# Attention statistics through a ring, and the scaling of probabilities one step later

## The reference

```
h = embed(x, position)
y = layernorm(h)
q, k, v = latent projections of y, with rope and rms norm      # 8 heads, 2 key/value heads, width 64
scores = einsum("bhqd,bhkd->bhqk", q, k) * 64 ** -0.5          # causal mask
attn_w = softmax(scores)
h = h + (einsum("bhqk,bhkd->bhqd", attn_w, v) + v_res) @ W_O
h = h + experts(layernorm(h))       # mean and variance of each token of h are needed here
```

## Time and profile before

| | |
|---|---|
| median of 3 runs | 2085.62 us (2084.45 to 2085.73) |
| the profiled execution | 2084.88 us |
| its span | 2083.0 us |
| TensorE busy | 1844.9 us (89%) |
| VectorE busy | 1828.0 us (88%) |
| ScalarE busy | 1454.8 us (70%) |
| GpSimd busy | 682.5 us (33%) |
| mean granted TensorE clock | 0.937 |
| `attend` in the trace | about 290 to 571 us |

### The profile page before, as it was taken

How to read it: one execution, slowest core, us unless ns; L and a number is a source line. 1 busy time by engine, 2 the same in 40 slices (tenths; PEclk the granted TensorE clock), 3 DMA queues, 4 the chain that set the end, 5 groups by cost and what they waited for, 6 DMA issues and landing times.

```text
span 2083.0 us, 29167 instructions
## 1 busy us (share of the span) xinstructions
PE 1844.9 (89%) x8486; PEld 1461.0 (70%) x8486; DVE 1828.0 (88%) x2358; ACT 1454.8 (70%) x2558; POOL 682.5 (33%) x439
## 2 busy tenths in 40 slices
PE   5455658878766999999999999999999999999998
PEld 3333335555554888888888888878888888888887
DVE  8435558888677999999999999979999999999997
ACT  2145546666522888888888888878888888888886
POOL 4250015445312233333333333323333333333330
PEclk9967769899955999999999999999999999999999
DMA  7410000000012333333333333323333333333331
GB/s 207 136 41 0 1 1 1 0 0 0 1 34 96 126 121 108 124 126 126 113 113 126 126 124 109 119 101 126 117 112 124 126 126 111 116 126 126 123 108 56
DMA packets 105256, 191.46 MB, mean 92 GB/s; under 512 B 13558, under 2 KB 86246, under 8 KB 88550
## 3 DMA queue, kind: packets, MB, share of 16 engines
q1 hardware_dynamic: 103166, 186.77, 26.1%
q0 software_dynamic: 2048, 4.20, 0.7%
HBM read 179.40 MB, written 11.53 MB: 92 GB/s over the span
## 4 chain that ended last, share of the span: by engine, by line
PE 67%; DVE 0%; issue 0%; ACT 0%; DVEq 0%; ACTq 0%
PE f_ps_h L1837 11%; PE f_ps_h L1838 11%; PE f_ps_h L1839 11%; PE f_ps_y L1848 11%; PE f_ps_y L1849 11%; PE f_ps_y L1850 11%; PE f_ps_y L1863 0%; DVE s_lo L1793 0%; DVE scaled L1787 0%; PE f_ps_h L1874 0%; ACT act_out L1748 0%; DVE h L1811 0%; ACT y_t L1772 0%; DVEq L1669 0%; PE f_ps_h L1819 0%
## 5 line engine op out<-in xcount | busy, mean ns | idle before, releaser
L1748 ACT ACTIVATE act_out<-f_ps_h,b_t 128x512 f32<-128x512 f32 x1024 | 649.6, 686 | 257.4 <-PE f_ps_h L1839 257.4
L1787 DVE TENSOR_TENSOR scaled<-act_out,c_row 128x1024 f32<-128x1024 f32 x512 | 753.0, 1471 | 42.7 <-ACT act_out L1748 42.2
L1793 DVE TENSOR_TENSOR s_lo<-scaled,s_hi 128x1024 fp32r<-128x1024 f32 x512 | 672.7, 1314 | 0.1
L1756 ACT ACTIVATE s_hi<-scaled 128x1024 fp32r<-128x1024 f32 x512 | 541.9, 1058 | 2.3 <-DVE scaled L1787 1.5
L1651 POOL CAST w_hi<-w_raw 128x512 fp32r<-128x512 f32 x128 | 200.7, 1568 | 909.8 <-PE f_ps_y L1850 898.0
L1837 PE MATMUL f_ps_h<-x_hi,w_hi 128*128 x1024 | 399.8, 390 | 2.2 <-DVE h L1811 1.5
L1848 PE MATMUL f_ps_y<-s_hi,w_hi 128*128 128x512 f32 x1024 | 398.7, 389 | 3.0 <-DVE s_lo L1793 3.0
L1838 PE MATMUL f_ps_h<-x_lo,w_hi 128*128 x1024 | 399.4, 390 | 0.0
L1839 PE MATMUL f_ps_h<-x_hi,w_lo 128*128 x1024 | 399.2, 390 | 0.0
L1850 PE MATMUL f_ps_y<-s_hi,w_lo 128*128 128x512 f32 x1024 | 398.4, 389 | 0.0
L1849 PE MATMUL f_ps_y<-s_lo,w_hi 128*128 128x512 f32 x1024 | 398.4, 389 | 0.0
(11 more groups left out here) (219 smaller groups left out, 1652.7 us busy)
## 6 DMA issues: line engine op xcount, KB each, us to landing
c_row<-comb_rows SPq DMA_DIRECT2D x128, 1024.0 KB, 4.8
w_raw<-in_w SPq DMA_DIRECT2D x256, 128.0 KB, 4.3
by_slot<-b_zeros SPq DMA_DIRECT2D x1, 3072.0 KB, 13.4
b_gauss_s<-by_slot SPq DMA_DIRECT2D x12, 256.0 KB, 5.3
mixed_rows<-b_mixed SPq DMA_DIRECT2D x12, 256.0 KB, 2.3
out<-h SPq DMA_DIRECT2D x8, 256.0 KB, 4.7
cent<-in_centers SPq DMA_DIRECT2D x1, 1536.0 KB, 7.1
neg_prec<-in_logvar SPq DMA_DIRECT2D x1, 1536.0 KB, 10.9
```

What stands on the lines that cost most here:

```text
L1748: last = act.activation(act_out[:, r % 2, c, :], ps_h[:, r % 2, c, :], ACT.Gelu, bias=b1_t[:, c, bass.ds(e, 1)])
L1756: act.activation(s_hi[:, r % RING], scaled[:, r % RING], ACT.Copy).then_inc(hi_ready, 1)
L1787: dve.tensor_tensor(scaled[:, r % RING], act_out[:, r % 2], c_row[:, k, g * GT:(g + 1) * GT].unsqueeze(1).broadcast_to([P, HC, GT]), ALU.m ...
L1793: dve.tensor_tensor(s_lo[:, r % RING], scaled[:, r % RING], s_hi[:, r % RING].bitcast(F32), ALU.subtract).then_inc(lo_ready, 1)
```

## The change

`statistics` keeps BN_STATS and BN_AGGR on VectorE, but BN_AGGR writes into one of four slots of a ring, `mv_ring`, and nothing waits behind it at once. ScalarE copies the whole ring (8 elements per partition) into `mv` every fourth step, at the head of steps 9, 13, ... 33, and once after the last step. BN_STATS waits also for the aggregate before, and the aggregate of slot 0 for the last copy of the ring. GpSimd's `norm_p` works in step u on unit u-3, no longer on u-2. TensorE's, ScalarE's and VectorE's other work is as it was.

```diff
-        mvt = sb("a_mvt", [P, 2])
+        mv_ring = sb("a_mv_ring", [P, 4, 2])
...
-        mv_step = sem("mv_step")
+        stats_ready = sem("stats_ready")
+        mv_ready = sem("mv_ready")
+        mv_copied = sem("mv_copied")
...
+            def copy_mv(u):
+                if in_range(u, UNITS):
+                    act.wait_ge(mv_ready, u + 4)
+                    act.activation(mv[:, bass.ds(u, 4), :], mv_ring[:], ACT.Copy).then_inc(mv_copied, 1)
+
             def step(u, r):
+                if r == 1:
+                    copy_mv(u - 9)
                 copy_p(u - 4, r, 0)
...
             all_steps(act, step)
+            copy_mv(UNITS - 4)
...
                 norm_qk(u + 2, (r + 2) % 4)
                 copy_v(u - 3, (r - 3) % 4)
-                norm_p(u - 2, (r - 2) % 4)
+                norm_p(u - 3, (r - 3) % 4)
...
-            def statistics(u):
+            def statistics(u, slot):
                 if in_range(u, UNITS):
-                    link = chained(dve, mv_step, u * 3)
                     hold(dve, y_added, u + 1)
-                    link(dve.bn_stats(stats[:], h[:, u, :]))
-                    link(dve.bn_aggr(mvt[:], stats[:]))
-                    link(dve.tensor_tensor(mv[:, u, :], mvt[:], mvt[:], ALU.max))
+                    if not isinstance(u, int) or u > 0:
+                        hold(dve, mv_ready, u)
+                    dve.bn_stats(stats[:], h[:, u, :]).then_inc(stats_ready, 1)
+                    if slot == 0:
+                        after(dve, mv_copied, u // 4)
+                    hold(dve, stats_ready, u + 1)
+                    dve.bn_aggr(mv_ring[:, slot, :], stats[:]).then_inc(mv_ready, 1)
```

More of the change, by code:

```diff
@@ L1275, in step @@
                 add_y(u - 5)
-                statistics(u - 5)
+                statistics(u - 5, (r - 5) % 4)
             all_steps(dve, step)
```

## The result

| | before | changed |
|---|---|---|
| median | 2085.68 us (2084.45 to 2085.87, 4 runs) | 2039.73 us (2036.94 to 2039.97, 4 runs) |
| ratio | | 0.9778, 95% interval 0.9763 to 0.9794 |
| span of the profiled execution | 2083.0 us | 2037.8 us |
| VectorE busy | 1828.0 us | 1773.0 us |
| TensorE busy | 1844.9 us | 1829.7 us |

The forecast was 2043.5 us, in a range from 2037 to 2058.

A forecast was written before the change was run, and what follows sets the result against it. VectorE leads in the attention stage, its copy to mv held by GpSimd's scaling. Pairs of 7.74 + 5.75 = 13.5 us instead of 16.65, with the edges, save 42.3 us: 2043.5 us, range 2037 to 2058.

The forecast's parts named there:

- The mechanism: VectorE's two-element copy to mv, up to 2968 ns, is held until GpSimd's norm_p ends; work behind it waits.
- The odd step: Attention step with twice the keys: 4.14+1.87+0.49+1.24 = 7.74 us from its score, set by TensorE.
- The even step: Attention step with half the keys: 5.75 us, set by GpSimd's scaling, which the next step's turn_p waits for.
- VectorE's own way: Even step, from copy_q through maximum, mask, add_y and BN_AGGR to the next copy_q: 5.4 us.
- The sum: Attention stage: 13 pairs at 13.5 us give −40.9; with step 31, startup and end, −42.3 us.
- The end of step 31: Last odd step: copy_o starts 6.2 us after its score instead of 8.3, −2.1 us.
- The startup: First steps of the stage: norm_p(1) now stands behind a norm_qk, +0.5 us at most.
- The end: After the last step, with ScalarE's eighth ring copy exposed, and the barrier: +0.2 us.
- GpSimd's move: Even step: norm_p on unit u-3 is late behind norm_qk's wait for turn_q; without this gate −5 us more.
- ScalarE's part: Eight ring copies, 0.2 us each taken (0 to 1.02); seven covered by odd-step idle, the eighth exposed.
- the rival's price: TensorE's clock drops to 1.2 GHz in every pair: about 1.7 us each, 23 in all, 2066 us; chance 0.07.
- The slower rival: VectorE's copies, maximum and mask held while norm_p runs: pair 18.6 against 16.65 us, +25 us, 2111 us; chance 0.03.

The follow-up runs named there:

- the reduce in its place: Kernel before the change, with VectorE's two-element TENSOR_TENSOR copy to mv replaced by a TENSOR_REDUCE over an axis of one; ratio to before 0.9788.
- the tensor_copy: Kernel before the change, with VectorE's two-element TENSOR_TENSOR copy to mv replaced by a tensor_copy; ratio to before 1.0004.
- the two-input kernel: Changed kernel plus a two-element TENSOR_TENSOR from SBUF on VectorE, behind the maximum of every step; ratio to the kernel before 0.9948.

## Why the prediction was right, point by point

**The mechanism** was right. The held copy was the loss; the reduce in its place shows it without the rest of the change, and the tensor_copy shows that the place is not the cause.

**The odd step** was forecast at 7.74 us, set by TensorE, and is 7.58. Every offset up to the start of `turn_p` is as worked out (4.14, 1.87, 0.49). The term that was mis-sized is the last: from `turn_p`'s start to the free TensorE I took 1.24 us, and it is 1.08 (409.61 to 410.69). I had added durations whose modelled ends overlap by more than I allowed; two starts, had I shown them, would have been safer.

**The even step** was forecast at 5.75 us with GpSimd's scaling late, and is 5.60 with just that wait (0.34 us before `turn_p`). `turn_p` follows the scaling by 0.06 us, where I had 0.1 to 0.2, and the score follows `turn_p` by 1.13 where I had 1.24. VectorE's own way, 5.4 us, is what the step takes when GpSimd's wait is gone: 5.40.

**The sum.** The pair is 13.14 and not 13.5 us, 4.7 us over 13 pairs. The end of step 31 came out as forecast: its `copy_o` starts at 501.03, 6.20 us after the score (6.2). The startup cost nothing where I had allowed 0.5: the first two pairs take 10.83 and 9.71 us, before 10.84 and 9.72. The end cost nothing either: from the last BN_AGGR to routing's first instruction, with ScalarE's last ring copy between, 0.74 us against 0.93. So the stage gave 47.6 us for 42.3 of the sum. Against it stand 2.6 us ahead of the stage, where the two kernels do not differ. The changed kernel's profile has a slow stretch of the clock in the embedding that the other has not. The same window in the kernel before, and in the changed one:

```profile
84.00:88.00 4.00, 4.00 (x39) 4.00 (x38) 2.09 (x4) 1.80 (x4) 0.00 (x0) 1.00 0.71 215
```

```profile
84.00:88.00 4.00, 4.00 (x23) 4.00 (x22) 1.38 (x2) 1.19 (x2) 0.00 (x0) 0.57 0.60 176
```

TensorE is busy for all of both, but gets through 23 matmuls in place of 39. At the last copy of this part (90.92 before, 93.27 now) 2.35 of the 2.61 us are there. Of these, 0.71 us stand already ahead of the slow stretch, at a copy behind a DMA (81.31 and 82.02), so the slow stretch is worth about 1.6. What set the drop off I did not try. One of the four runs, 2036.94 us, lies about as much below the others, which fits a drop that comes in some executions only; this was not shown. That the time came within 4 us of the forecast is in part luck: the stage gave 5 us more than its sum, and 2.6 us that have nothing to do with the change hid half of that. Without them the time would have been about 2037 us, the lower edge of the range.

**GpSimd's move** I called what is late next, and gave 5 us for it. Its price is 3.3 us of the stage, shown twice: by undoing it, and by taking away the wait ahead of it. Nor does ScalarE's part cost anything in the loop: of its eight ring copies only the last, behind the last step, waits for its aggregate.

**The rivals.** The clock did not drop: it is 1.00 from 320 to 495 us. I gave no row for the rival's price, 1.7 us a pair; the two-input kernel shows 0.7 to 1.1, and what a slow stretch would cost in the changed kernel was not measured. Every slow stretch of the loops came with a long idle of TensorE ahead of it (2.63 us in the two-input kernel, 1.6 to 2.1 us before), while the gaps of 0.2 to 0.4 us in the changed kernel set off none in 175 us. The Trainium skill ("TensorE: Matmul & The Clock Gate", A second HAM failure mode) speaks of frequent micro-idles that make the clock oscillate; that is not borne out here at this size of gap. But the long idle alone does not decide: two pairs of the two-input kernel have the same 2.63 us and no drop, and neither has the kernel before from 420 to 498 us, with idles of 1.64 to 2.12 us in each pair. What else it takes is open. In the kernel before the drops cost nothing that shows: neighbouring pairs alternate between 16.55 and 16.91 us, with and without them. Two windows of that kernel, the first with drops (columns as in the earlier trace rows):

```profile
347.00:420.00 73.00, 62.65 (x412) 42.86 (x413) 62.52 (x84) 47.28 (x165) 36.08 (x27) 0.88 0.00 1
420.00:498.00 78.00, 59.55 (x438) 40.82 (x435) 67.46 (x89) 50.56 (x169) 40.17 (x29) 1.00 0.00 0
```

The slower rival needed maximum, mask or copies to be held. None is; what would be held is shown by the added instruction, and with it most of the gain is gone.

## What to carry to other kernels

A VectorE instruction whose time varies by a factor of eighteen at one size is waiting inside its duration; look for an instruction of GpSimd that ends when it ends. While GpSimd multiplies tensors in SBUF, as the scaling does here, keep instructions with two SBUF inputs and SBUF-to-SBUF copies off VectorE, however small, or give them another form (a reduce over an axis of one took 155 ns, and ScalarE's copy 198 ns). Only the scaling was seen to hold anything here. When a stall goes, walk each engine's way around the loop to find which is next: here the three ways of the even step, 5.05, 5.40 and 5.60 us, were all seen, each when the longer one was taken away. And a change made of two remedies should be tried one by one.

## What I had not expected of the hardware

- A copy of two elements is held for up to 2.98 us, to the end of GpSimd's instruction, as a tensor_copy just as well as with two inputs; the same two elements through a reduce take 0.155 us.
- In the kernel with the move only, a copy that began at 411.70 ran its 0.16 us although `norm_qk` began at 411.81, and so in every even step of the loop. It looks as if what has begun is not held, but the two overlap by 0.05 us on a timeline whose GpSimd times are rough, so this is not shown.
- The attention stage takes the same time on two chips to 0.1 us (267.50 in the kernel before here, 267.56 with the tensor_copy there), while the kernel before differs by 23 us between them. In these two profiles `copy_far` of step 1 starts at 302.90 here and at 328.63 there, and what follows the stage takes 1512.6 us in both, so the difference lies ahead of the stage.
